# Gathered rows and one-hot tables of a graph kernel: three bf16 parts in place of one fp32 value

## What is computed

```python
h = maximum(layernorm(x), 0)
Xs = h[src]
msg = where(edge_type == 0, Xs @ W_data.T + b_data, Xs @ W_control.T + b_control)
x = x + relu(segment_sum(msg, dst) + h @ W_self.T + b_self)
h = maximum(layernorm(x), 0)
deg = segment_sum(1, dst);  norm = rsqrt(deg)[src] * rsqrt(deg)[dst]
out = y = h
for _ in range(2):
    y = segment_sum(y[src] * norm, dst)
    out = out + y
return x + out / 3
```

## Time and profile before

| | us |
|---|---|
| median of 3 runs | 4849.11 (4844.41 to 4851.61) |
| profiled execution, first to last instruction (span) | 4840.8 |
| PE busy | 3663.3 (76%) |
| PEld busy | 3001.0 (62%) |
| DVE busy | 1959.6 (40%) |
| ACT busy | 2307.7 (48%) |
| POOL busy | 2869.0 (59%) |
| mean granted TensorE clock | 0.728 |

### The profile page before, as it was taken

One profiled execution on the slowest core, in us unless ns is written; L12 is line 12 of the kernel. 1 busy time (PEld: TensorE's weight loads), 2 busy tenths in 40 slices (PEclk: granted clock), 3 DMA queues, 4 the chain that ended last, 5 costly groups with the idle time before them and its releaser, 6 DMA issues. The chain is left out here.

```text
span 4840.8 us, 59773 instructions
## 1 busy us (share of the span) xinstructions
PE 3663.3 (76%) x22243; PEld 3001.0 (62%) x22243; DVE 1959.6 (40%) x3213; ACT 2307.7 (48%) x3075; POOL 2869.0 (59%) x3055
## 2 busy tenths in 40 slices
PE   7345766677667767666767699898897789998898
PEld 4334444444444444434444688888887688888888
DVE  7213666666666667667666011111112111111111
ACT  4001433333333434334334566666666566666666
POOL 2666665666665666666664556655663565655654
PEclk9555555555555555555556799999998899999999
DMA  5222332323232323233233455555555455555554
GB/s 186 58 53 67 95 92 87 107 90 91 91 107 91 91 91 105 92 95 107 92 103 97 123 149 153 154 156 150 154 151 168 130 148 139 145 144 146 145 144 132
DMA packets 367258, 571.63 MB, mean 118 GB/s; under 512 B 66678, under 2 KB 308225, under 8 KB 359283
## 3 DMA queue, kind: packets, MB, share of 16 engines
q1 hardware_dynamic: 270435, 370.74, 24.4%
q0 software_dynamic: 95664, 196.60, 16.1%
q10 hardware_dynamic: 864, 0.39, 0.0%
HBM read 424.48 MB, written 142.99 MB: 117 GB/s over the span
## 5 line engine op out<-in xcount | busy, mean ns | idle before, releaser
L863 POOL DMA_INDIRECT rows<-typed_table,index x1661 | 1584.4, 954 | 953.6 <-issue 503.1
L863 POOL DMA_INDIRECT rows<-hop_table,index x1306 | 1246.4, 954 | 943.3 <-PE sums_bank L1079 471.2
L999 ACT CAST strip_ring<-stage 128x1792 fp32r<-128x1792 uint8 x840 | 1376.3, 1685 | 751.4 <-remote 384.2
L1188 PE MATMUL wide<-table_parts,strip_ring 128*128 128x256 f32 x11760 | 1567.2, 296 | 112.4 <-issue 60.2
L1188 PEld LDWEIGHTS wide<-table_parts,strip_ring 128*128 128x128 f32 x11760 | 1525.7, 204 | 130.6 <-issue 108.3
L990 ACT CAST stage<-wide 128x392 uint8<-128x392 f32 x1920 | 801.3, 502 | 1356.1 <-PE wide L1150 878.4
L1079 PE MATMUL sums_bank<-hot,rows 128*128 128x80 f32 x5934 | 1095.1, 347 | 291.4 <-issue 240.9
L1150 PE MATMUL wide<-stage 128*128 128x392 bf16 x1920 | 755.1, 490 | 671.6 <-ACT stage L990 309.8
L1079 PEld LDWEIGHTS sums_bank<-hot,rows 128*128 128x128 f32 x5934 | 1047.1, 263 | 328.7 <-issue 325.5
L1150 PEld LDWEIGHTS wide<-stage 128*128 128x128 bf16 x1920 | 185.6, 110 | 1196.7 <-ACT stage L990 525.2
L1550 DVE TENSOR_TENSOR stage<-count_up,stage 128x1568 bf16<-128x1568 f32 x480 | 851.3, 1773 | 0.0
(11 more groups left out here) (140 smaller groups left out, 936.4 us busy)
## 6 DMA issues: line engine op xcount, KB each, us to landing
stage<-strips SPq DMA_DIRECT2D x840, 224.0 KB
strips<-stage SPq DMA_DIRECT2D x60, 1568.0 KB
rows<-typed_table,index POOLq DMA_INDIRECT x1661
rows<-hop_table,index POOLq DMA_INDIRECT x1306
hop_table<-scaled SPq DMA_DIRECT2D x50, 256.0 KB
resid<-xin SPq DMA_DIRECT2D x50, 256.0 KB
xin<-resid SPq DMA_DIRECT2D x50, 256.0 KB
typed_table<-rows SPq DMA_DIRECT2D x49, 256.0 KB, 2.1
```

The lines of the kernel that those rows point to most:

```text
L863: pool.indirect_dma_start(out=rows[:, o % RING, c, :], out_offset=None, in_=tables[k], in_offset=bass.IndirectOffsetOnAxis(ap=index[:, chu ...
L999: act.copy(strip_ring[:, number % STRIP_RING], counts_ring[place]).then_inc(strip_cast, 1)
L1188: last = pe.matmul(wide[:, nth % 4, 0:PARTS * P], strip_ring[:, number % STRIP_RING, b - first, :], table_parts[:, b, :, :].rearrange("p n ...
```

## The change

Every value that is gathered by edge is stored as three bf16 numbers (high, middle, low) whose sum is the fp32 value: high is the value rounded to bf16, middle the rounded rest, low the rest of that. A row is 768 bytes, not 512. The one-hots of the groups become bf16, so that a chunk is three bf16 matmuls instead of one fp32 matmul, which the program issues as two instructions. `before_cell`, `all_twos` and `batch_degree` become bf16 too.

The splits cost instructions. In the preparation each pair's messages go VectorE (bias), ScalarE (high), VectorE (rest), ScalarE (middle), GpSimd (low), with five message buffers and four rest buffers. GpSimd's six index steps move in between. In `finish` of the gather pass and of the first hop, ScalarE copies the high part, VectorE subtracts, ScalarE copies the middle part, VectorE subtracts again. The split has one buffer, in `own_in` in the gather pass and in `late_split` in the first hop. The first hop also stores its fp32 values (`hop_values`), which the reload reads. The buffer `fresh` is gone: the values are worked on in `scaled`. SP stores a finished batch at the head of a slot, ahead of the slot's strip loads. The reload ring has 2 places, not 3.

```diff
-MESSAGES = 6
+MESSAGES = 5
+RESTS = 4
+EXACT = 3
+SOURCE_STEPS = (6, 9, 12, 15, 19, 23)
-RELOAD_RING = 3
+RELOAD_RING = 2
@@ tables and rings
-        rows = sbuf("rows", [RING, CHUNKS, P])
-        hot = sbuf("hot", [RING, CHUNKS, WINDOW])
+        rows = sbuf("rows", [RING, CHUNKS, row_parts], BF16)
+        hot = sbuf("hot", [RING, CHUNKS, WINDOW], BF16)
@@ SP, store_nodes
-                    sp.wait_ge(scaled_ready, n + 1)
-                    sp.dma_start(of_batch(tables[k + 1], s), in_blocks(scaled[:, n % 2, :])).then_inc(table_stored[n % 2], 16)
                     sp.wait_ge(resid_ready, n + 1)
                     sp.dma_start(of_batch(resid, s), in_blocks(xin[:, n % XIN, :])).then_inc(resid_stored[n % XIN], 16)
+                    if k == 1 and not general:
+                        sp.wait_ge(scaled_ready, n + 1)
+                        sp.dma_start(of_batch(hop_values, s), in_blocks(scaled[:, n % 2, :])).then_inc(values_stored[n % 2], 16)
+                    sp.wait_ge(split_ready, n + 1)
+                    sp.dma_start(of_batch(tables[k + 1], s), split_of(k, general)).then_inc(table_stored, 16)
@@ POOL, preparation
+            for i in range(pairs):
+                pool.wait_ge(message_middle, i + 1)
+                message = messages[i % MESSAGES]
+                pool.tensor_tensor(message[:, :, :, 2, :], rests[i % RESTS], message[:, :, :, 1, :], ALU.subtract).then_inc(message_ready, 1)
+                if i in SOURCE_STEPS:
+                    source_step(SOURCE_STEPS.index(i))
@@ ACT, preparation
+            def take_high(i):
+                act.wait_ge(message_made, i + 1)
+                if i >= MESSAGES:
+                    act.wait_ge(message_stored[i % MESSAGES], 16 * (i // MESSAGES))
+                act.copy(messages[i % MESSAGES][:, :, :, 0, :], rests[i % RESTS]).then_inc(message_high, 1)
+
+            def take_middle(i):
+                act.wait_ge(message_rest, i + 1)
+                act.copy(messages[i % MESSAGES][:, :, :, 1, :], rests[i % RESTS]).then_inc(message_middle, 1)
@@ ACT, finish (now in the first hop too)
+                split = split_of(k, general)
+                act.wait_ge(scaled_ready, n + 1)
+                if n:
+                    act.wait_ge(table_stored, 16 * n)
+                act.copy(split[:, :, 0:P], in_blocks(values)).then_inc(split_high, 1)
+                if k == 0 and not general:
+                    act.copy(table_parts[:, first:first + blocks, 0, :], in_blocks(values[:, 0:blocks * P], blocks)).then_inc(high_ready, 1)
+                act.wait_ge(split_rest, n + 1)
+                act.copy(split[:, :, P:2 * P], in_blocks(scaled[:, (n + 1) % 2, :])).then_inc(split_middle, 1)
@@ PE, sum_rows
-                    last = pe.matmul(sums_bank[:, bank, 0:columns], rows[:, slot, c, :], hots[:, c, :],
-                                     start=(c == 0), stop=(c == size - 1))
+                    for n in range(EXACT):
+                        last = pe.matmul(sums_bank[:, bank, 0:columns], rows[:, slot, c, n * P:(n + 1) * P], hots[:, c, :],
+                                         start=(c == 0 and n == 0), stop=(c == size - 1 and n == EXACT - 1))
@@ DVE, preparation
+            def leave_rest(i):
+                dve.wait_ge(message_high, i + 1)
+                dve.tensor_tensor(rests[i % RESTS], rests[i % RESTS], messages[i % MESSAGES][:, :, :, 0, :], ALU.subtract
+                                  ).then_inc(message_rest, 1)
@@ DVE, finish
+                split, rest = split_of(k, general), in_blocks(scaled[:, (n + 1) % 2, :])
+                dve.wait_ge(split_high, n + 1)
+                dve.tensor_tensor(rest, in_blocks(scaled[:, n % 2, :]), split[:, :, 0:P], ALU.subtract).then_inc(split_rest, 1)
+                if k == 0 and not general:
+                    part_low(s * NODE_BLOCKS, blocks, in_blocks(values, blocks), high_ready, n + 1, low_ready)
+                dve.wait_ge(split_middle, n + 1)
+                dve.tensor_tensor(split[:, :, 2 * P:3 * P], rest, split[:, :, P:2 * P], ALU.subtract).then_inc(split_ready, 1)
```

More of the change, by code:

```diff
@@ L495, in count_of, with values_need, split_of @@
             return (n - place + ring - 1) // ring if n > place else 0
-        def table_need(k):
-            return [16 * count_of(k * total, 2, parity) for parity in range(2)]
+        def values_need(n):
+            return 16 * (count_of(n + 1, 2, n % 2) - count_of(total, 2, n % 2))
+        def split_of(k, general):
+            return early_split if k == 0 and not general else late_split
         def event_at(k, slot):
@@ L807, in _ @@
                                     load_event(k, *event_at(k, slot))
[L808 to L812 removed]
+                        if leaving and leaving == event_at(k, events[k][-1][0]):
+                            load_counts_behind(number for at in range(slots_of(k), slots_of(k) + LAST) for number in steps_at(k, at))
                         if coming:
@@ L880, in _ @@
                         pool.wait_ge(index_halved, 1)
-                        for parity in range(2):
-                            pool.wait_ge(table_stored[parity], table_need(k)[parity])
+                        pool.wait_ge(table_stored, 16 * k * total)
                     with pool.Fori(0, groups) as g:
@@ L957, in _, with finish @@
                 copy_h(i)
+                if i >= 1:
+                    take_high(i - 1)
+                if i >= 2:
+                    take_middle(i - 2)
                 if load_measured(i - 2):
                     root(load_measured(i - 2))
-            def finish(n, k, s, splits):
+            take_high(pairs - 1)
+            take_middle(pairs - 2)
+            take_middle(pairs - 1)
+            def finish(n, k, s, general):
+                first, blocks = s * NODE_BLOCKS, held(s)
+                values = scaled[:, n % 2, :]
                 if k == 0:
@@ L980, in _ @@
                         act.copy(ring_index[:, :], index[:, ds(g * CHUNKS, CHUNKS)]).then_inc(rest_index, 1)
-                    for s in range(total):
-                        finish(k * total + s, k, s, False)
+                    for s in range(total if k < HOPS else 0):
+                        finish(k * total + s, k, s, True)
                 act.nop()
@@ L1085, in count_edges @@
                 for c in range(size):
-                    upper = hots[:, c, :].bitcast(BF16).rearrange("p (w t) -> p w t", t=2)[:, :, 1]
-                    last = pe.matmul(sums_bank[0:1, bank, P:P + columns], one_short[:, 0:1], upper,
+                    last = pe.matmul(sums_bank[0:1, bank, P:P + columns], one_short[:, 0:1], hots[:, c, :],
                                      start=(c == 0), stop=(c == size - 1))
@@ L1313, in _ @@
                                     ).then_inc(edges_copied, 1)
+            leave_rest(pairs - 1)
             dve.wait_ge(edges_copied, 2 * rounds)
@@ L1360, in _ @@
             dve.tensor_tensor(pair_tile[:, :, 1], scratch[0], scratch[1], ALU.add).then_inc(pairs_made, 1)
+            dve.memset(scaled[:, :, :], 0.0)
             dve.wait_ge(filled, 5)
@@ L1376, in take_degrees, with finish @@
                 dve.tensor_scalar(spread_now[:, 1, :], degree, 1.0, None, ALU.max).then_inc(degree_read, 1)
-            def finish(n, k, s, source, turn, splits, own=None):
+            def finish(n, k, s, source, turn, general, own=None):
                 blocks = held(s)
@@ L1582, in read_tile @@
                                       ).then_inc(tile_read, 1)
+                dve.wait_ge(message_ready, pairs)
                 make_hot(0)
```

153 lines of the change are left out of this document (90 added, 63 removed).

## The result

The changed kernel takes 4926.5 us (4919.1 to 4932.4, 4 runs), the kernel before 4846.8 us. The ratio is 1.0172 (95% interval 1.0151 to 1.0193): slower by 1.7%, where 4435 us, 8.5% faster, and a range of 4250 to 4720 had been predicted. The profiled execution spans 4923.9 us against 4840.8.

A forecast was written before the change was run, and what follows sets the result against it. It took the ring-freeing loop to bound the gather pass and TensorE the hops: span 4840.8 + 27 (preparation) - 268 (gather pass) - 172 (hops) = 4428; runs' median 8.3 above, rounded to 4435 us. Range 4250 to 4720.

The forecast's parts named there:

- What bounds the gather pass: Gather pass: bound by the loop that frees ring buffers, not by gathers; a group costs it some 6.6 us.
- the chain 12.04 - 1.94: Gather pass: cheaper sums cut a slot's chain to 10.10 us; with batches and GpSimd's floor 10.75, saving 268 us.
- Size of the sums: Sums: 24 bf16 instructions a group take 1.6 us at half clock, 0.9 at full, as lower bound.
- rival C: Hops: bf16 load and matmul pair, 0.08 us, no faster per group; only gather pass pays, 4633 us; chance 0.13.
- The upper cost of 2.6 us: Sums in gather pass: weight load counted as half an fp32 one, 2.6 us a group, saving put at 0.97.
- Gathers of 768 bytes cost GpSimd nothing: Gathers: rows grow from 512 to 768 bytes, but GpSimd's time isn't per byte, so no added cost.
- In the hops TensorE is the bound: Both hops: TensorE sets the time, busy 854 of 974 and 960 of 1101 us.
- Hops, stall "about as it is, 1.1 us": Hop sums: idle time in a group stays about 1.1 us, group becomes 2.25 us, saving 197 us.
- Rival D: Hop sums and early gather-pass slots: stalls by issue paid per instruction, slower, 5181 us; chance 0.06.
- ScalarE's queue in the first hop, and the second gap: First hop: batch casts queued ahead of strip casts make TensorE wait, 16 + 9 us, counted as +25.
- Preparation: Preparation: ScalarE's two casts make a pair 2.5 us instead of 1.95, +27 us, bounds +10 and +60.
- Rival B: Gather pass and hops: VectorE and ScalarE take over the loop, 2.5 us delay perhaps not fp32's; 4634 us; chance 0.22.

The follow-up runs named there:

- e12: Changed kernel without exactness: one bf16 part in tables and rows, 8 matmuls a group, one cast a batch, no subtractions; 0.969 of the kernel before.
- e14: Kernel before, nothing left out, with a 320-byte memset behind each gather, about 1.49 us apart; 0.962 of the kernel before.
- e1: Changed kernel, TensorE sums only the high part of each row, 8 matmuls a group for 24, rows still 768 bytes; 0.978 of the kernel before.
- e4: Changed kernel without making the middle and low parts in preparation and batches; rows, gathers and sums kept; 0.993 of the kernel before.
- e3: Kernel before with 256-byte rows gathered for 512 in gather pass and first hop, second hop untouched; 0.999 of the kernel before.

## Why the prediction was wrong

- **What bounds the gather pass** (first part, and the chain 12.04 - 1.94 in "Gather pass"): the step that failed. I took 6.6 us of a slot for the group's own chain and let it shrink with the matmuls; 268 us were expected from it and 17.5 came. In all 15 traces with eight gathers started 1.21 to 1.50 us apart and the cells complete, with 8, 16 or 24 matmuls, 256 to 768 bytes, 64 or 128 rows, a slot took 11.75 to 12.2 us (pass / 207.6); with four gathers it took 8.3 to 9.0. The number of gathers sets it. The 2.0 us that GpSimd "waits for sums" are not TensorE's work (with a third of the matmuls the slot is 11.9 us): the completions come late while gathers follow each other at 1.25 us, and GpSimd waits for what its own gathers hold. At 1.50 us the wait is 0 and the completions are prompt. "The pass isn't bound by gathers" read GpSimd's instruction time of 1.257 us as the price of a gather.
- **Size of the sums** (1.6 us a group): right. 24 bf16 matmuls went in 1.5 us at half clock between starts, and in 1.03 at full clock, 0.043 us each. That is half of rival C's 0.08. (The upper cost of 2.6 us would have saved 3.54 - 2.6 = 0.9 us a slot, where I wrote 0.97.) By the Trainium skill, "TensorE: Matmul & The Clock Gate", section on LDWEIGHTS, 24 loads of 128 columns would take 2.6 us (an estimate, 24 times that page's 107 ns); 1.03 measured is against it and agrees with the section on weight-path perf modes, by which such a bf16 load is read faster. Its back-to-back gap of about 81 ns is for 128 moving columns; with 80 it wasn't reached.
- **Gathers of 768 bytes cost GpSimd nothing**: right (0.958 us).
- **"In the hops TensorE is the bound"**: only in part. The second hop, first to last gather, takes 979 us or more in every run with eight gathers, 12 us a slot, though e12's sums cost 1.1 us a group and e14's 2.9 with the waits for rows; with four gathers it takes 760 to 834 us. Saved TensorE time partly turned into waits for strip casts (e1).
- **Hops, stall "about as it is, 1.1 us"**: wrong in size, 1.47. Gain per group 0.35 to 0.4 us in place of 1.2. Rival D named the sign, TensorE idle by "issue" and more of it with more instructions, but neither its size (1.7 us a group lost) nor its cause. With the gathers spaced the stall is 0.06.
- **ScalarE's queue in the first hop, and the second gap** (+25 us): right in mechanism, too small. TensorE's waits for strip casts there grew from 28 to 109 us, by 81. First hop and second gap are 63 us longer while the second hop, with the same groups, is 21 shorter. I counted late tiles and left out the transition, where reloads and two batches follow each other and TensorE waits 21 us.
- **Preparation** (+27, bound +60): I named ScalarE as the bound at 2.5 us a pair. ScalarE is busy 64 of 98 us. The fullest is VectorE, busy 84% before, which got 41 us; a pair took 3.0 us (bias adds from 20 to 166 us). Without the second and third part 46 of the 58 us went (e4). What GpSimd's index steps between the subtractions of a ring of four add isn't shown apart. +58, at the bound.
- **Rival B** said that the 2.5 us delay may not belong to fp32. It was the right doubt; it made VectorE and ScalarE the successors, and those take over only with half the gathers.
- **Clock**: 0.61 in the pass after, 0.55 before; it rose, so it explains none of the loss.

In sum: the saved TensorE time was real, 330 us in the pass alone, and lay under the gathers; the price, +58 in the preparation and +65 in first hop and gaps, lay on the path. Not settled: through what gathers in flight hold TensorE's instructions and completions (bytes, rows and GpSimd's own work are excluded as the main part, the dependence on their number and spacing is shown, a queue of transfers isn't seen), and why the change costs 1.7% on the first chip and nothing on another. Not tried: a ring of more than four row buffers, which might hide late completions, and a spacing made by something other than a memset.

## What to carry to other kernels

When an engine "waits for" another one's result and both have room, look whether the result was late or only its arrival: compare the last instruction's start with the waiter's, once with the waiter's own traffic in flight and once without. Before making the sums cheaper, slow the supplier down on purpose: here one small memset behind each gather gave 3.8 to 4.8% on the kernel before, and with it both forms of the sums took the same second hop. Of a new chain of casts and subtractions, count what each step puts on the engine that is busiest at that stage, not on the one that has most of the steps.

## What the hardware showed that I had not expected

- Gathers issued every 1.25 us held TensorE in steps of 0.7 us, in which instructions without any wait stood still, and delayed its completions, by 2.6 to 4.0 us at the median of the late ones. From 1.50 us apart on this was gone (idle time in a group 1.03 us to 0.03 before, 1.47 to 0.06 after). At 1.21 us with half the rows it was 0.88. The transfers themselves were no slower at 1.25 us than at 1.50: rows landed 2.2 to 2.3 us after a gather's start.
- The slot of eight gathers, 11.75 to 12.2 us or 1.5 us a gather, didn't depend on 256, 512 or 768 bytes a row.
- Chips differ in this: the kernel before took 4847 to 4861 us in three sets and 4977 to 5019 in three others, with its second hop 1045.5 us long on the first chip and 1106.5 on one of the slow ones (e3, where that hop is untouched).
